# Five of 32 state groups of a selective scan take another route: u replicated by DMA and multiplied on GpSimd, decay in PSUM; products with C two groups at a time

## The chip, the cores and the metric

The kernel runs on one NeuronCore of a Trainium2 chip. The metric is the device time of one launch in microseconds (us). Engines are named as in the profile: PE (TensorE), DVE (VectorE), ACT (ScalarE), POOL (GpSimd) and SP (SyncE, which here only issues DMAs). SPq and ACTq are the DMA issues of SP and ACT.

## What is computed

Two layers follow each other on x of shape 4 x 128 x 64 x 64. The first (attention over 4096 positions and a layer norm) is not touched by the change. The second adds a 3x3 convolution, a spectral convolution and a Mamba block. The change is inside the scan of the Mamba block:

```python
def step(h, inp):                       # one position; h is 256 channels x 16 states
    xt, dtt, Bt, Ct = inp
    dA = jnp.exp(dtt[..., None] * A)
    h = dA * h + dtt[..., None] * Bt[:, None, :] * xt[..., None]
    y = jnp.einsum('bdn,bn->bd', h, Ct)
    return (h, y)
```

With u = dt * x, each of the 256 x 16 = 4096 states h is a recurrence over the positions: h = exp(dt A) h + u B, and y sums h C over the 16 states of a channel.

## The kernel before

The second layer (`layer1`) handles 32 items one after the other: 4 images times 8 chunks (STEPS) of LC = 512 positions. The 4096 states of an item are 32 groups g = 0 to 31 of 128 rows: 8 channels (GC) times 16 states (ST). For each group the engines do this, in this order of dependence:

- SP, `load_dt` (L959): a DMA reads the 8 rows of dt of the group from DRAM (`dt_dram`) and writes each of them to 16 partitions, 256 KB into one of 16 buffers of `d_a` (NDA).
- ACT, `decay` (L1207): d_a = exp(a_neg * d_a), in place, in SBUF.
- PE, `repeat_u` (L1098): one matmul spreads the 8 rows of u to 128 rows in one of 4 PSUM banks (NU).
- DVE, `times_b` (L1255): that bank times B, in place.
- DVE, the scan (L1269): hh = scan of d_a and the bank, into one of 8 buffers (NHH). It reads one operand in SBUF and one in PSUM.
- ACT, `last_state` (L1200): the last column is kept for the next chunk.
- POOL (L1300): hc = hh * c_rep, into one of 8 buffers (NHC).
- PE, `sum_states` (L1080): for four groups at a time, sums over the states into PSUM.

Each engine has its own list written out by hand, and they meet only at semaphores. DVE's order is times_b(g + 1), scan(g), times_b(g + 2), scan(g + 1) and so on. Between the groups each engine also does `prepare`: the projections, activations and tables of item it + 1. On POOL these are ux = dt * xs at g = 13 (L1287), lo_u at g = 17 (L1291) and two gates per item (L1282). u goes to PE as a high and a low part: `hi_u`, and `lo_u`, which ACT places by two DMAs (`place_low`, L1148) into the other half of the partitions of `s_u`.

SP's list per item, step t = 0 to 31, waits for scan t and then issues the load of group t + 16 (for t of 16 and more, group t - 16 of the next item). At t = 16 it first stores dt of the next item to DRAM (`store_dt`, L953, 512 KB) and waits until that has landed before the next load (L957). At t = 6 and 8 it loads the next chunks of the layer's input (`za`, `stage_j`, `zp`), and at t = 18 it stores an output chunk (L948). The last item also issues the 16 loads that a further item would need, and SP's list ends with a wait for all DMAs.

Of the kernel before, what the change touches and what calls it, by code (L numbers as in the profile page):

```python
# [7 lines left out]
ACT = mybir.ActivationFunctionType  # L8
# [745 lines left out]
def layer1(nc, z_ext, w, out, nb=B):  # L754
# [13 lines left out]

    NIT = nb * STEPS
    dt_dram = nc.dram_tensor("dt_dram", [2, INNER, LC], F32, kind="Internal").ap()  # L770
    with ExitStack() as ctx:
        def sb(name, shape, dt=F32):
            return ctx.enter_context(nc.sbuf_tensor(name, shape, dt))
# [51 lines left out]
        d_a = sb("d_a", [128, NDA, LC])  # L825
        hh = sb("hh", [128, NHH, LC])
        hc = sb("hc", [128, NHC, LC])


        loaded, mixed, a_exp, carry_zero, row_zero, halved = [sem(n) for n in (  # L830
# [2 lines left out]
        with nc.Block() as block:  # L833
# [27 lines left out]
            def _(dve):  # L861
# [27 lines left out]
             "hi_ready", "lo_ready", "u_rep", "da_ready", "bu_ready", "scanned", "kept", "hc_ready", "y_done",  # L889
             "y_added", "gated", "z_used", "o_ready", "o_copied", "o_full", "o_even", "o_odd", "dt_stored", "u_placed")]  # L890
        dt_in = [sem(f"dt_in{i}") for i in range(NDA)]


        XS, XD, DT, BI, CI, GATE, GI, NITEM = 0, 2, 3, 5, 6, 7, 9, 10
# [13 lines left out]
        def channels(g):  # L908

            half, jj, i = g // 16, g // 4 % 4, g % 4  # L910
            return 128 * half + 32 * i + GC * jj

        def steps(prepare, emit, tail):

# [6 lines left out]
        with nc.Block() as block:  # L921
            @block.sync
            def _(sp):
                def load(j):

                    p, b, lc = j % 2, j % NIT // STEPS, j % STEPS
                    if j >= 2:
                        sp.wait_ge(item, (j - 2) * NITEM + GI + 1)
                    ge(sp, flipped, 2 * j)
                    sp.dma_start(za[:, p, :], z_ext[b, :, bass.ds(lc * LC, HALO)]).then_inc(z_in, 16)  # L930

                    last = (STEPS - 1 - lc) * LC + W
                    sp.dma_start(stage_j[:, 0:ROWS - 1, :], z_ext[b, :, bass.ds(last + W, LC - W)].rearrange("c (h w) -> c h w", w=W)).then_inc(z_in, 16)
                    sp.dma_start(stage_j[:, ROWS - 1, :], z_ext[b, :, bass.ds((STEPS - lc) % STEPS * LC + W, W)]).then_inc(z_in, 16)

                def load_padded(j):

                    p, b, lc = j % 2, j // STEPS, j % STEPS
                    ge(sp, z_used, j - 1)
                    sp.dma_start(zp[:, p, :, 1:W + 1], z_ext[b, :, bass.ds(lc * LC, HALO)].rearrange("c (h w) -> c h w", w=W)).then_inc(zp_in, 16)  # L940

                def store(j, p):
                    b, lc = j // STEPS, j % STEPS
                    if lc == 0:
                        sp.wait_ge(o_full, b + 1)
                    else:
                        sp.wait_ge(o_copied, j + 1)
                    sp.dma_start(out[b, :, bass.ds(lc * LC, LC)], o_sb[:, p, :]).then_inc((o_even, o_odd)[p], 16)  # L948

                def store_dt(j, p):  # L950

                    sp.wait_ge(item_read, j * NITEM + DT + 2)
                    sp.dma_start(dt_dram[p].rearrange("(h q) l -> q h l", h=2), dt[:, :, :]).then_inc(dt_stored, 16)  # L953

                def load_dt(j, p, g):
                    if g == 0:
# [32 lines left out]
                sp.wait_ge(u_placed, 32 * (NIT + 1))  # L989
                sp.wait_ge(o_even, 16 * (NIT // 2))  # L990
                sp.wait_ge(o_odd, 16 * (NIT // 2))
                for i in range(NDA):
                    sp.wait_ge(dt_in[i], 16 * (NIT * G // NDA + 1))
                sp.wait_ge(z_in, 48 * (NIT + 1))

            @block.tensor
            def _(pe):
# [128 lines left out]
            def _(act):  # L1126
# [76 lines left out]
                def decay(it, g):  # L1203

                    s, j = column(g)
                    act.wait_ge(dt_in[g % NDA], it * (16 * G // NDA) + 16 * (g // NDA) + 16)
                    nc.scalar.activation(d_a[:, g % NDA, :], d_a[:, g % NDA, :], ACT.Exp,  # L1207
                                         scale=a_neg[:, s * 8 + j:s * 8 + j + 1]).then_inc(da_ready, 1)
# [33 lines left out]
            def _(dve):  # L1242
# [4 lines left out]

                def times_b(it, p, g):

                    dve.wait_ge(u_rep, it * G + g + 1)  # L1250
                    if g == 0:
                        dve.wait_ge(item_read, it * NITEM + BI + 1)

# [3 lines left out]
                def emit(it, p):  # L1257
                    times_b(it, p, 0)
                    for g in range(G):

                        if g + 1 < G:
                            times_b(it, p, g + 1)
                        s, j = column(g)
                        dve.wait_ge(bu_ready, it * G + g + 1)
                        dve.wait_ge(da_ready, it * G + g + 1)

                        ge(dve, hc_ready, it * G + g - NHH + 1)
                        ge(dve, kept, it * G + g - NHH + 1)
                        nc.vector.tensor_tensor_scan(hh[:, g % NHH, :], d_a[:, g % NDA, :], ps[:, U_BANK + g % NU, :],  # L1269
                                                     carry[:, it % STEPS, s * 8 + j:s * 8 + j + 1], ALU.mult, ALU.add).then_inc(scanned, 1)  # L1270
                        if g == 16 and it and (it - 1) % STEPS == 0:
                            add_row(it - 1, 1 - p)
# [6 lines left out]
            def _(pool):  # L1279
# [4 lines left out]
                def prepare(j, p, g):  # L1284
                    if g == 13:
                        pool.wait_ge(item_read, j * NITEM + DT + 2)
                        pool.tensor_tensor(ux[:, :, :], dt[:, :, :], xs[:, p, :, :], ALU.mult).then_inc(u_prod, 1)  # L1287
                    elif g == 17:
                        pool.wait_ge(hi_ready, j * 3 + 1)
                        ge(pool, u_placed, j * 32)  # L1290
                        pool.tensor_tensor(lo_u[:, :, :], ux[:, :, :], hi_u[:, :, :].bitcast(F32), ALU.subtract).then_inc(lo_ready, 1)  # L1291

                def emit(it, p):
                    for g in range(G):
                        pool.wait_ge(scanned, it * G + g + 1)
                        if g == 0:
                            pool.wait_ge(item_read, it * NITEM + CI + 1)
# [4 lines left out]
                        if g == 22:  # L1302
                            gate(it, p, 0)
                        if g == 6 and it:
                            gate(it - 1, 1 - p, 1)

                def tail():
# [83 lines left out]
```

## Time and profile before

| | before |
|---|---|
| median of 3 runs | 5654.49 us |
| lowest and highest run | 5650.64 and 5657.19 us |
| the profiled execution's own time | 5656.6 us |
| its span in the trace | 5654.8 us |
| granted TensorE clock over the span | 0.983 |
| share of the span: PE, DVE, ACT, POOL | 94%, 88%, 69%, 83% |
| DMA | 549.14 MB, 97 GB/s over the span |

The execution's own time is 1.8 us more than its span. The first layer takes the first two thirds of the span. The second layer's first scan starts at 3825.7 us, and the last DMA of the program is issued at 5650.5 us. The shares are averages over both layers, so they don't tell what limits the second; the stretches of time below do. The DMA share in a stretch is the mean busy share of the core's 16 DMA engines, and it can come out slightly above 1, as packets overlap.

### The profile page before, as it was taken

What the parts mean: (1) busy time and instruction counts of PE and PEld (TensorE: products, weight loads), DVE (VectorE), ACT (ScalarE), POOL (GpSimd) and SP (SyncE); (2) the same over time, 40 slices, a digit from 0 to 9 for tenths busy, and PEclk for the clock granted to TensorE, in tenths of its full rate; (3) what the DMA queues carried; (4) which work ended last, traced back from release to release, by engine and by line L of the source; (5) the groups of instructions that cost most, each with busy time, mean ns of one, the idle gap of its engine ahead of it and who ended that gap; (6) DMA issues with size and microseconds to landing.
All of it is one profiled execution on the core that took longest, in us unless ns stands there. A gap on an engine that the chain in (4) does not pass through costs nothing. (4 is left out here: it accounts for less than half of the span.)

```text
span 5654.8 us, 81519 instructions
## 1 busy us (share of the span) xinstructions
PE 5338.5 (94%) x25264; PEld 2432.7 (43%) x25264; DVE 4949.7 (88%) x7220; ACT 3876.3 (69%) x7513; POOL 4692.7 (83%) x3661
## 2 busy tenths in 40 slices
PE   7999999999999999999999999968888888888888
PEld 3444444444444444444444444423333333333333
DVE  6888888888888888888888888829999999999998
ACT  3666666666666766666666666657777777777776
POOL 4888887888888788888788888747888888888887
PEclk8999999999999999999999999989999999999999
DMA  4111122211111211112211010225555555555555
GB/s 139 36 53 50 37 61 71 60 55 38 46 49 64 79 39 53 45 40 62 64 54 33 18 32 21 67 84 196 186 190 188 188 187 189 186 188 190 186 188 174
DMA packets 337475, 549.14 MB, mean 97 GB/s; under 512 B 76016, under 2 KB 99568, under 8 KB 335600
## 3 DMA queue, kind: packets, MB, share of 16 engines
q1 hardware_dynamic: 327536, 526.62, 28.8%
q10 hardware_dynamic: 9504, 17.31, 1.1%
q8 instruction: 202, 3.31, 0.2%
q14 instruction: 233, 1.91, 0.1%
HBM read 415.10 MB, written 109.84 MB: 93 GB/s over the span
## 5 line engine op out<-in xcount | busy, mean ns | idle before, releaser
L649 DVE TENSOR_REDUCE mpart<-ps 128x1 f32<-128x512 f32 x4096 | 2539.1, 682 | 536.4 <-PE ps L406 535.8
L533 ACT ACTIVATE exps<-ps 128x512 f32<-128x512 f32 x4096 | 2146.8, 600 | 1139.8 <-PE ps L413 1114.1
L406 PE MATMUL ps<-k_st,q_ring 96*128 96x512 f32 x4096 | 1778.2, 435 | 20.2 <-DMA k_st<-qk_split 15.6
L413 PE MATMUL ps<-q_ring,k_st 98*128 98x512 f32 x4096 | 1621.5, 397 | 3.8 <-ACT exps L533 3.4
L1300 POOL TENSOR_TENSOR hc<-hh,c_rep 128x512 f32<-128x512 f32 x1024 | 1295.8, 1278 | 310.8 <-DVE hh L1269 291.8
L1269 DVE TENSOR_TENSOR_SCAN hh<-d_a,carry,ps 128x512 f32<-128x512 f32 x1024 | 1311.9, 1284 | 0.0
L622 POOL TENSOR_TENSOR held<-exps 128x512 f32<-128x512 f32 x768 | 987.7, 1311 | 359.9 <-ACT exps L533 359.9
L406 PEld LDWEIGHTS ps<-k_st,q_ring 96*128 96x128 f32 x4096 | 774.7, 189 | 1136.5 <-DVE mpart L649 685.2
L622 POOL TENSOR_TENSOR sums<-exps 128x512 f32<-128x512 f32 x896 | 1134.5, 1282 | 72.0 <-ACT exps L533 70.0
L424 PE MATMUL ps<-exps,v_ring 128*32 128x512 f32 x8192 | 1092.4, 605 | 0.0
L413 PEld LDWEIGHTS ps<-q_ring,k_st 98*128 98x128 f32 x4096 | 778.3, 190 | 139.7 <-ACT exps L533 18.0
L1098 PE MATMUL ps<-s_u,sel_g 128*128 128x512 f32 x1024 | 573.6, 565 | 219.3 <-DVE hh L1269 213.9
L1255 DVE TENSOR_TENSOR ps<-ps,b_rep 128x512 f32<-128x512 f32 x1024 | 701.5, 688 | 37.0 <-PE ps L1098 37.0
L1207 ACT ACTIVATE d_a<-d_a,a_neg 128x512 f32<-128x512 f32 x1024 | 731.1, 720 | 3.4 <-DMA d_a<-dt_dram 1.4
L1098 PEld LDWEIGHTS ps<-s_u,sel_g 128*128 128x128 f32 x1024 | 193.5, 189 | 824.0 <-DVE hh L1269 689.3
L622 POOL TENSOR_TENSOR second<-exps 128x512 f32<-128x512 f32 x384 | 493.1, 1284 | 56.0 <-POOL sums L622 0.9
L626 POOL TENSOR_TENSOR sums<-sums,second 128x512 f32<-128x512 f32 x384 | 492.2, 1282 | 30.1
L672 DVE TENSOR_REDUCE held_sum<-held 128x128 f32<-128x768 f32 x512 | 482.0, 942 | 6.0 <-POOL held L622 6.0
L1200 ACT COPY carry<-hh 128x1 f32<-128x1 f32 x1024 | 186.1, 182 | 251.3 <-DVE hh L1269 251.3
L424 PEld LDWEIGHTS ps<-exps,v_ring 128*32 128x32 f32 x8192 | 161.3, 108 | 419.4 <-ACT exps L533 364.3
L1014 PE MATMUL ps<-za,wtap 128*128 128x512 f32 x528 | 274.6, 614 | 26.9 <-DMA stage_j<-z_ext 26.9
L1080 PE MATMUL ps<-hc,sel_y 128*32 128x512 f32 x2048 | 293.6, 647 | 5.4 <-POOL hc L1300 5.4
(113 smaller groups left out, 3881.3 us busy)
## 6 DMA issues: line engine op xcount, KB each, us to landing
d_a<-dt_dram SPq DMA_DIRECT2D x1040, 256.0 KB
qk_split<-hilo SPq DMA_DIRECT2D x128, 256.0 KB, 2.3
out_dram<-out_sb SPq DMA_DIRECT2D x128, 256.0 KB, 2.0
heads_in<-out_dram SPq DMA_DIRECT2D x32, 1024.0 KB, 5.2
q_ring<-qk_split SPq DMA_DIRECT2D x384, 64.0 KB, 2.0
k_st<-qk_split SPq DMA_DIRECT2D x45, 512.0 KB, 7.4
dt_dram<-dt SPq DMA_DIRECT2D x33, 512.0 KB, 5.5
s_u<-lo_u ACTq DMA_DIRECT2D x66, 256.0 KB, 5.9
```

Source lines behind the costliest of these rows:

```text
L406: nc.tensor.matmul(d_bank(("max", m, t)), q_ring[0:PARTS, m % 4, 128 * i:128 * i + 128], k_st[0:PARTS, g % 2, chunk(kc)], start=True, stop ...
L413: nc.tensor.matmul(a_bank(("exp", n, t)), k_st[0:SHIFT, n // NCH % 2, 128 * t:128 * t + 128], q_ring[0:SHIFT, n % 4, :], start=True, stop= ...
L424: ins = nc.tensor.matmul(ps[D * i:D * i + D, OUT_BANK, :], v_ring[:, n // NCH % 2, 4 * v + i, :], exps[:, (2 * v + i // 2) % EXPS, CH * (i ...
L533: nc.scalar.activation(exps[:, u % EXPS, CH * half:CH * half + CH], a_bank(("exp", n, t)), ACT.Exp, scale=SCALE).then_inc(a_done, 1)
L622: pool.tensor_tensor(dst, exps[:, u % EXPS, 0:CH], exps[:, u % EXPS, CH:2 * CH], ALU.add).then_inc(summed, 1)
L626: pool.tensor_tensor(unit, unit, second[:, :], ALU.add).then_inc(summed, 1)
L649: nc.vector.tensor_reduce(mpart[:, m % 2, t % 4, t // 4:t // 4 + 1], d_bank(("max", m, t)), AX.X, ALU.max).then_inc(d_done, 1)
L1098: nc.tensor.matmul(ps[:, U_BANK + g % NU, :], sel_g[:, j, :], s_u[:, p, s, :], start=True, stop=True).then_inc(u_rep, 1)
L1207: nc.scalar.activation(d_a[:, g % NDA, :], d_a[:, g % NDA, :], ACT.Exp, scale=a_neg[:, s * 8 + j:s * 8 + j + 1]).then_inc(da_ready, 1)
L1255: nc.vector.tensor_tensor(bu, bu, b_rep[:, p, :], ALU.mult).then_inc(bu_ready, 1)
L1269: nc.vector.tensor_tensor_scan(hh[:, g % NHH, :], d_a[:, g % NDA, :], ps[:, U_BANK + g % NU, :], carry[:, it % STEPS, s * 8 + j:s * 8 + j ...
L1300: pool.tensor_tensor(hc[:, g % NHC, :], hh[:, g % NHH, :], c_rep[:, p, :], ALU.mult).then_inc(hc_ready, 1)
```

## The change

Five groups of each item (SPREAD = 6, 11, 21, 25 and 29) take another route. The other 27 are handled as before.

- SP stores u of the next item to DRAM at t = 19 (`store_u`, 512 KB), and loads each of the five groups' u with `load_u`: 8 rows, each written to 16 partitions, 256 KB into one of 3 buffers `su` (NSU). In form this DMA is that of `load_dt`. The loads are issued at t = 6, 11, 21, 25 and 29. The one at t = 21 is the first for the next item and waits until its u has landed in DRAM.
- POOL multiplies `su` by B in place (`spread_b`), ahead of the product with C that it stands before in POOL's list.
- ACT writes the decay of these groups to the PSUM bank that `repeat_u` would have filled, two steps later in its list than before, after the scan of group g - 4.
- PE leaves out `repeat_u` and DVE leaves out `times_b` for the five. Their scans read the decay from PSUM and u B from SBUF.
- For all groups, POOL's product with C covers two groups (128 x 1024) with c_rep repeated by a zero stride. It starts when the second of the two is scanned, and `hc_ready` counts pairs.
- ux is written only after the previous u is stored.

```diff
+    SPREAD = (6, 11, 21, 25, 29)
+    NSP, NSU = len(SPREAD), 3
 SP
+                def store_u(j, p):
+                    sp.wait_ge(u_prod, j + 1)
+                    sp.dma_start(u_dram[p].rearrange("(h q) l -> q h l", h=2), ux[:, :, :]).then_inc(u_stored, 16)
+                def load_u(m):
+                    j, g = m // NSP, SPREAD[m % NSP]
+                    if j >= NIT:
+                        return
+                    sp.wait_ge(u_stored, j * 16 + 16)
+                    if m >= NSU:
+                        sp.wait_ge(scanned, (m - NSU) // NSP * G + SPREAD[(m - NSU) % NSP] + 1)
+                    c = channels(g)
+                    sp.dma_start(su[:, m % NSU, :], u_dram[j % 2, c:c + GC, :].rearrange("c (o l) -> c o l", o=1).to_broadcast([GC, ST, LC])
+                                 ).then_inc(su_in[m % NSU], 16)
...
+                        if t == 19:
+                            store_u(it + 1, 1 - p)
+                        for m in LOADS.get(t, ()):
+                            load_u(it * NSP + m)
...
+                LOADS = {SPREAD[0]: (3,), SPREAD[1]: (4,), SPREAD[2]: (5,), SPREAD[3]: (6,), SPREAD[4]: (7,)}
...
                 for g in range(NDA):
                     load_dt(0, 0, g)
+                store_u(0, 0)
+                for m in range(NSU):
+                    load_u(m)
 PE
-                    pe.wait_ge(hc_ready, it * G + 4 * n + 4)
+                    pe.wait_ge(hc_ready, it * G // 2 + 2 * n + 2)
...
-                        repeat_u(it, p, g)
+                        if g not in SPREAD:
+                            repeat_u(it, p, g)
 ACT
+                    if g in SPREAD:
+                        act.wait_ge(scanned, it * G + g - NU + 1)
+                        nc.scalar.activation(ps[:, U_BANK + g % NU, :], d_a[:, g % NDA, :], ACT.Exp,
+                                             scale=a_neg[:, s * 8 + j:s * 8 + j + 1]).then_inc(spread_da, 1)
...
-                        decay(it, g)
+                        if g not in SPREAD:
+                            decay(it, g)
...
+                        if g - 2 in SPREAD:
+                            decay(it, g - 2)
 DVE
-                        if g + 1 < G:
+                        if g + 1 < G and g + 1 not in SPREAD:
                             times_b(it, p, g + 1)
...
+                        a, bu = d_a[:, g % NDA, :], ps[:, U_BANK + g % NU, :]
+                        if g in SPREAD:
+                            m = spread(it, g)
+                            dve.wait_ge(spread_bu, m + 1)
+                            dve.wait_ge(spread_da, m + 1)
+                            a, bu = bu, su[:, m % NSU, :]
 POOL
+                def spread_b(it, p, g):
+                    m = spread(it, g)
+                    pool.wait_ge(su_in[m % NSU], 16 * (m // NSU) + 16)
+                    pool.tensor_tensor(su[:, m % NSU, :], su[:, m % NSU, :], b_rep[:, p, :], ALU.mult).then_inc(spread_bu, 1)
...
-                    for g in range(G):
+                    for g in range(1, G, 2):
...
+                        for w in SPREAD:
+                            if (w - 4) // 2 == g // 2:
+                                spread_b(it, p, w)
...
-                        pool.tensor_tensor(hc[:, g % NHC, :], hh[:, g % NHH, :], c_rep[:, p, :], ALU.mult).then_inc(hc_ready, 1)
+                        pool.tensor_tensor(hc[:, g % NHC - 1:g % NHC + 1, :], hh[:, g % NHH - 1:g % NHH + 1, :],
+                                           c_rep[:, p, :].rearrange("p (o l) -> p o l", o=1).to_broadcast([128, 2, LC]), ALU.mult).then_inc(hc_ready, 1)
```

## Rows read from the trace of the kernel before

**Rows 1.** The page: span and the busy time of the engines.

```profile
span 5654.8 us, 81519 instructions
...
PE 5338.5 (94%) x25264; PEld 2432.7 (43%) x25264; DVE 4949.7 (88%) x7220; ACT 3876.3 (69%) x7513; POOL 4692.7 (83%) x3661
```

**Rows 2.** One item's length by windows: the engines, granted clock, DMA share, GB/s.

```profile
core 0: us, PE busy (x) PEld busy (x) DVE busy (x) ACT busy (x) POOL busy (x), PEclk, DMA share, GB/s
4826.50:4883.14 56.64, 50.08 (x181) 20.10 (x180) 56.64 (x65) 42.85 (x89) 47.24 (x37) 0.97 0.58 187
```

**Rows 3.** Timeline of DVE over the end of an item: start, length, operation.

```profile
4842.59 1.27 DVE L1269 TENSOR_TENSOR_SCAN hh<-d_a,carry,ps 128x512 f32<-128x512 f32 x1
4843.77 0.67 DVE L1255 TENSOR_TENSOR ps<-ps,b_rep 128x512 f32<-128x512 f32 x1
4844.36 2.44 DVE L1269 TENSOR_TENSOR_SCAN hh<-d_a,carry,ps 128x512 f32<-128x512 f32 x2
4846.72 1.27 DVE L1255 TENSOR_TENSOR ps<-ps,b_rep 128x512 f32<-128x512 f32 x2
```

**Rows 4.** Timeline of POOL around ux, in an item.

```profile
4815.91 2.37 POOL L1287 TENSOR_TENSOR ux<-dt,xs 128x1024 f32<-128x1024 f32 x1
4818.24 3.73 POOL L1300 TENSOR_TENSOR hc<-hh,c_rep 128x512 f32<-128x512 f32 x3
```

**Rows 5.** What SP waited for, 4100 to 5400 us: total us, times, longest.

```profile
SPq L959 <- DVE hh L1269: 668.2, 613, 4.2
SPq L957 <- DMA dt_dram<-dt: 119.3, 23, 7.2
```

**Rows 6.** The page's DMA issues: count, KB of one, us to landing.

```profile
d_a<-dt_dram SPq DMA_DIRECT2D x1040, 256.0 KB
...
dt_dram<-dt SPq DMA_DIRECT2D x33, 512.0 KB, 5.5
s_u<-lo_u ACTq DMA_DIRECT2D x66, 256.0 KB, 5.9
za<-z_ext SPq DMA_DIRECT2D x33, 320.0 KB, 4.1
zp<-z_ext SPq DMA_DIRECT2D x32, 320.0 KB, 7.1
...
out<-o_sb SPq DMA_DIRECT2D x32, 256.0 KB, 7.3
stage_j<-z_ext SPq DMA_DIRECT2D x33, 224.0 KB, 4.1
...
stage_j<-z_ext SPq DMA_DIRECT2D x33, 32.0 KB, 4.9
```

**Rows 7.** Windows inside one item, columns as in Rows 2; the last two are DMA's.

```profile
4820.00:4821.00 1.00, 1.00 (x3) 0.44 (x3) 1.00 (x2) 1.00 (x3) 1.00 (x2) 1.00 1.02 373
4838.00:4850.00 12.00, 9.84 (x51) 4.92 (x50) 12.00 (x15) 7.43 (x20) 8.53 (x8) 1.00 0.53 200
4823.00:4826.50 3.50, 3.50 (x15) 1.21 (x14) 3.50 (x5) 0.55 (x2) 3.50 (x3) 1.00 0.13 46
4826.50:4853.50 27.00, 24.02 (x100) 10.95 (x99) 27.00 (x32) 20.41 (x45) 21.89 (x18) 1.00 0.58 197
4854.50:4861.50 7.00, 5.91 (x21) 2.18 (x20) 7.00 (x9) 6.93 (x13) 5.46 (x5) 1.00 0.47 147
```

**Rows 8.** Timeline of SP's DMA issues around the store of dt.

```profile
4818.77 0.47 SPq L953 DMA_DIRECT2D dt_dram<-dt  x1
4824.80 1.21 SPq L959 DMA_DIRECT2D d_a<-dt_dram  x2
```

**Rows 9.** The start of the scans: SP's first loads and DVE's first scan.

```profile
3810.91 25.55 SPq L959 DMA_DIRECT2D d_a<-dt_dram  x22
...
3825.74 1.27 DVE L1269 TENSOR_TENSOR_SCAN hh<-d_a,carry,ps 128x512 f32<-128x512 f32 x1
```

**Rows 10.** The last DMA issue of the program, by SP's timeline.

```profile
5650.48 0.35 SPq L948 DMA_DIRECT2D out<-o_sb  x1
```

More of the change, by code:

```diff
@@ L770, in layer1 @@
     dt_dram = nc.dram_tensor("dt_dram", [2, INNER, LC], F32, kind="Internal").ap()
+    u_dram = nc.dram_tensor("u_dram", [2, INNER, LC], F32, kind="Internal").ap()
+    SPREAD = (6, 11, 21, 25, 29)
+    NSP, NSU = len(SPREAD), 3
     with ExitStack() as ctx:
@@ L827, in layer1 @@
         hc = sb("hc", [128, NHC, LC])
+        su = sb("su", [128, NSU, LC])
         loaded, mixed, a_exp, carry_zero, row_zero, halved = [sem(n) for n in (
@@ L891, in layer1 @@
         dt_in = [sem(f"dt_in{i}") for i in range(NDA)]
+        su_in = [sem(f"su_in{i}") for i in range(NSU)]
+        u_stored, spread_da, spread_bu = [sem(x) for x in ("u_stored", "spread_da", "spread_bu")]
         XS, XD, DT, BI, CI, GATE, GI, NITEM = 0, 2, 3, 5, 6, 7, 9, 10
@@ L911, in channels, with by_pe, spread @@
             return 128 * half + 32 * i + GC * jj
+        def by_pe(it, g):
+            return it * (G - NSP) + g - sum(1 for w in SPREAD if w < g)
+        def spread(it, g):
+            return it * NSP + SPREAD.index(g)
         def steps(prepare, emit, tail):
@@ L989, in _ @@
                 sp.wait_ge(u_placed, 32 * (NIT + 1))
+                sp.wait_ge(u_stored, 16 * (NIT + 1))
                 sp.wait_ge(o_even, 16 * (NIT // 2))
@@ L1206, in decay @@
                     act.wait_ge(dt_in[g % NDA], it * (16 * G // NDA) + 16 * (g // NDA) + 16)
-                    nc.scalar.activation(d_a[:, g % NDA, :], d_a[:, g % NDA, :], ACT.Exp,
-                                         scale=a_neg[:, s * 8 + j:s * 8 + j + 1]).then_inc(da_ready, 1)
+                    if g in SPREAD:
+                        act.wait_ge(scanned, it * G + g - NU + 1)
+                        nc.scalar.activation(ps[:, U_BANK + g % NU, :], d_a[:, g % NDA, :], ACT.Exp,
+                                             scale=a_neg[:, s * 8 + j:s * 8 + j + 1]).then_inc(spread_da, 1)
+                    else:
+                        nc.scalar.activation(d_a[:, g % NDA, :], d_a[:, g % NDA, :], ACT.Exp,
+                                             scale=a_neg[:, s * 8 + j:s * 8 + j + 1]).then_inc(da_ready, 1)
                 def emit(it, p):
                     for g in range(G):
-                        decay(it, g)
+                        if g not in SPREAD:
+                            decay(it, g)
                         if g >= KEEP:
@@ L1248, in times_b @@
                 def times_b(it, p, g):
-                    dve.wait_ge(u_rep, it * G + g + 1)
+                    dve.wait_ge(u_rep, by_pe(it, g) + 1)
                     if g == 0:
@@ L1259, in emit @@
                     for g in range(G):
-                        if g + 1 < G:
+                        if g + 1 < G and g + 1 not in SPREAD:
                             times_b(it, p, g + 1)
                         s, j = column(g)
-                        dve.wait_ge(bu_ready, it * G + g + 1)
-                        dve.wait_ge(da_ready, it * G + g + 1)
-                        ge(dve, hc_ready, it * G + g - NHH + 1)
+                        a, bu = d_a[:, g % NDA, :], ps[:, U_BANK + g % NU, :]
[4 more added lines that the diff above has]
+                            a, bu = bu, su[:, m % NSU, :]
+                        else:
+                            dve.wait_ge(bu_ready, by_pe(it, g) + 1)
+                            dve.wait_ge(da_ready, by_pe(it, g) + 1)
+                        if it * G + g >= NHH:
+                            dve.wait_ge(hc_ready, (it * G + g - NHH) // 2 + 1)
                         ge(dve, kept, it * G + g - NHH + 1)
-                        nc.vector.tensor_tensor_scan(hh[:, g % NHH, :], d_a[:, g % NDA, :], ps[:, U_BANK + g % NU, :],
+                        nc.vector.tensor_tensor_scan(hh[:, g % NHH, :], a, bu,
                                                      carry[:, it % STEPS, s * 8 + j:s * 8 + j + 1], ALU.mult, ALU.add).then_inc(scanned, 1)
@@ L1286, in prepare @@
                         pool.wait_ge(item_read, j * NITEM + DT + 2)
+                        ge(pool, u_stored, j * 16)
                         pool.tensor_tensor(ux[:, :, :], dt[:, :, :], xs[:, p, :, :], ALU.mult).then_inc(u_prod, 1)
@@ L1291, in prepare @@
                         pool.tensor_tensor(lo_u[:, :, :], ux[:, :, :], hi_u[:, :, :].bitcast(F32), ALU.subtract).then_inc(lo_ready, 1)
+                def spread_b(it, p, g):
+                    m = spread(it, g)
+                    pool.wait_ge(su_in[m % NSU], 16 * (m // NSU) + 16)
+                    pool.tensor_tensor(su[:, m % NSU, :], su[:, m % NSU, :], b_rep[:, p, :], ALU.mult).then_inc(spread_bu, 1)
                 def emit(it, p):
-                    for g in range(G):
+                    for g in range(1, G, 2):
+                        if g == 1:
+                            pool.wait_ge(item_read, it * NITEM + CI + 1)
+                        for w in SPREAD:
+                            if (w - 4) // 2 == g // 2:
+                                spread_b(it, p, w)
                         pool.wait_ge(scanned, it * G + g + 1)
-                        if g == 0:
-                            pool.wait_ge(item_read, it * NITEM + CI + 1)
                         ge(pool, y_done, it * 8 + (g - NHC) // 4 + 1)
-                        pool.tensor_tensor(hc[:, g % NHC, :], hh[:, g % NHH, :], c_rep[:, p, :], ALU.mult).then_inc(hc_ready, 1)
+                        pool.tensor_tensor(hc[:, g % NHC - 1:g % NHC + 1, :], hh[:, g % NHH - 1:g % NHH + 1, :],
+                                           c_rep[:, p, :].rearrange("p (o l) -> p o l", o=1).to_broadcast([128, 2, LC]), ALU.mult).then_inc(hc_ready, 1)
                         prepare(it + 1, 1 - p, g)
-                        if g == 22:
+                        if g == 23:
                             gate(it, p, 0)
-                        if g == 6 and it:
+                        if g == 7 and it:
                             gate(it - 1, 1 - p, 1)
```

## The prediction, made before the changed kernel ran

> **What bounds the kernel now.** I read the page first, then cut the second layer into stretches of one item, then followed single queues. On the page PE leads with 94%, but that mixes two layers [rows 1]. In one item of the second layer, 56.64 us, the row says something else: DVE is busy for 56.64 of 56.64 us, PE for 50.08, POOL for 47.24 and ACT for 42.85 [rows 2]. The reader is to see DVE without a hole and nobody else so. The timeline of DVE shows the pace: from the start of a scan to the start of the next times_b is 4843.77 - 4842.59 = 1.18 us, from there to the next scan 4844.36 - 4843.77 = 0.59 us. Together 1.77 us a group, and 32 x 1.77 = 56.6 us an item. Two scans in a row, which occur at the end of an item, start 2.44 - 1.27 = 1.17 us apart, so a scan costs 1.18 us whatever follows it [rows 3].
>
> The view that decides is that of the DMA engines, though. While only loads of d_a run, they move 200 GB/s at a share of 0.53; while the store of dt runs beside them, 373 GB/s at a share of 1.02 [rows 7]. I read this so: a load of d_a uses 8 of the 16 DMA engines, all of them fully, and that half can do no more than 200 GB/s. A load of 262,144 bytes then costs 1.31 us of that half. It has 8 source rows. The Trainium skill says why, on its page "DMA: Bandwidth & Descriptors", section "Why a DMA increments its semaphore by 16 and not by 1": a transfer is split over the largest number of engines up to 16 that divides the slowest dimension of both sides, which is 8 here. By this rule the trace's half share is the full rate of such a load.
>
> **The busy half of the DMA engines, before.** Per item it gets all of the 32 loads, 32 x 256 = 8192 KB, and half of what else moves: dt 512, za 320, zp 320, stage_j 224 + 32, out 256 and s_u 2 x 256, so 2176 / 2 = 1088 KB [rows 6]. That is 9280 KB = 9.50 MB, or 47.5 us at 200 GB/s. A stretch of an item shows what this misses: from 4826.5 to 4853.5 us, 27.0 us, the mean share is 0.58, over the 0.53 of a full half, and 197 x 27.0 = 5.32 MB move [rows 7]. Out and s_u are in it, 768 KB = 0.79 MB, half of it on the other engines, so the busy half carries 4.93 MB, 24.6 us at 200 GB/s. It took 2.4 us longer. With that the item's work is 47.5 + 2.4 = 49.9 us.
>
> To it comes a forced hole. SP issues the store of dt at 4818.77 and the next load at 4824.80 [rows 8], after waiting for the landing; 23 items of a long stretch lose 119.3 / 23 = 5.2 us of SP in this wait [rows 5]. In the 3.5 us from 4823.0 to 4826.5 the share is 0.13 [rows 7], a hole of 3.5 x (1 - 0.13 / 0.53) = 2.6 us. The half is full again by 4826.5, so packets come at most 1.7 us after the issue at 4824.80; I take 1.3. So the half is taken for 49.9 + 2.6 = 52.5 of 56.64 us. From above: after 4854.5 loads run at 147 GB/s, DVE's pace of one in 1.77 us, idle for 7 x (1 - 147 / 200) = 1.85 us [rows 7]; 56.64 - 1.85 - 2.6 = 52.2 us of work is thus the most there can be. SP's wait for scans, 668.2 us in 1300 [rows 5], only says that SP isn't the limit; it issues, and the work piles up behind it.
>
> **The change part by part.**
> DVE loses five times_b per item, 5 x 0.59 = 2.95 us, 53.7 us are left [rows 3]. The operands of the five scans change places, still one in SBUF and one in PSUM; I take the scan's price as unchanged.
> PE loses five matmuls and was 6.6 us under DVE; no cost.
> POOL, by start to start: a product takes 1.24 us ((3.73 - 1.27) / 2), ux 2.33 us (4818.24 - 4815.91) [rows 4]. The trace has no product with a repeated operand. Below it is bounded by ux's 2.33 us for 1024 columns, above by two single products, 2.48; I take 2.33, as it has the same count of elements. POOL's item becomes 16 x 2.33 + 5 x 1.24 (spread_b) + 2 x 1.24 (gates) + 2 x 2.33 (ux, lo_u) = 50.6 us, at most 53.0. Either is under 53.7. Its backlog is longest after ux, lo_u and three spread_b: from group 13 to 25 it has six pairs 14.0, ux and lo_u 4.7, gate 1.2 and three spread_b 3.7, 23.6 us, while DVE takes 12 x 1.77 - 2 x 0.59 = 20.1 us. So it is some 3.5 us behind; hh and hc have 8 buffers, over 10 us. Hidden.
> ACT writes five decays to PSUM rather than SBUF, same count; it has 13.8 us free per item. Hidden.
> DMA gains five loads of 256 KB on the busy half and a store of 512 KB, half of it there: 1536 KB = 1.57 MB, 7.9 us per item. The new wait for u's landing has two loads issued behind the store (t = 20 and 21), 2.6 us of work, about the time from the store's last packet to the next load's first; I price this second hole at 0, and at most 2.6.
>
> **The sum.** The busy half needs 49.9 + 7.9 + 2.6 = 60.4 us per item. That is above DVE's 53.7 and above the 56.64 of before. The loads, not the scans, then set the pace: SP falls behind the scans, decays wait for d_a, scans for decays. Bounds: without the 2.4 us 57.9 ; with the most work 52.2 + 7.9 + 2.6 = 62.7.
> Now the whole. The first loads are issued at 3810.91 [rows 9], packets from 3812.2. Then 16 loads 21.0, s_u 1.3, store of u 1.3, a hole 2.6, three loads of u 3.9: the items' loads begin at 3842.3. 31 items of 60.4 make 1872.4. The last has no loads of z and three of u less: 60.4 - 2.3 - 3.9 = 54.2. That is 5768.9; the useless loads at the end count too, since SP waits for them. From the last issue to the end of the span were 4.3 us [rows 1, 10]; I add 3, as the last load is issued before its turn. Span 5771.9, its own time 1.8 more, 5773.7, against 5656.6 of the profiled run: +117. The profiled run was 2.1 above the median, so 5771.6; I say 5770. By the bounds: 57.9 gives 31 x 2.5 + 2.5 = 80 less, 5690; 62.7 gives 74 more, 5844.
>
> **The rivals.**
> DVE stays the bound, the other sign. This is so if loads of u cost the busy half little, that is if the half isn't a hard limit: the point from which it decides is 53.7 us of DMA per item, 6.7 less than my sum. For it: nobody waits for d_a now, and SP mostly waits for scans. Against it: 12 us at exactly 200 GB/s while DVE's pace asks for 148. It gives 32 x 2.95 = 94.4 less. At the start u of group 6 lands late: 3812.2 + 21.0 + 1.3 + 1.3 + 2.6 + 1.3 and about 0.5, plus 1.24 on POOL, is 3841.4, while the scan was due at 3825.74 + 6 x 1.77 - 0.59 = 3835.8: 5.6 more. At the end the last pair starts with its second group, 1.1 + 1.1 more. 5654.5 - 94.4 + 5.6 + 2.2 = 5568. The same DMA page, "Specifications", gives a fabric ceiling of 435 GB/s over 16 engines. As an estimate from it, an item's 12.4 MB (all of the KB above, with the change's) would need 29 us, and this rival would hold. The trace's 200 GB/s of loads alone speaks against its use here.
> DMA is the bound, but lighter: the hole is filled and the 2.4 us aren't there. 47.5 + 7.9 = 55.4 us an item: 1.2 under before, 5654.5 - 38 = about 5615.
> POOL is the bound: it would need a pair of over 2.52 us to pass 53.7, ((53.7 - 13.3) / 16), and over 2.94 to pass 60.4. At 2.7 us alone it would be 56.5 us, no change. Both inputs and the count speak against it.
>
> **How the numbers follow.** DMA as the bound, between 57.9 and 62.7 us an item: 0.74. DVE as the bound: 0.13. Light DMA: 0.08, spread on both sides of no change, 0.04 faster, 0.03 the same, 0.01 slower. POOL: 0.05, split 0.02, 0.02 and 0.01. A measurement of this kernel tells 0.2%, 11 us, from no change. Faster 0.13 + 0.04 + 0.02 = 0.19, same 0.03 + 0.02 = 0.05, slower 0.74 + 0.01 + 0.01 = 0.76. The likeliest case's own range is 5690 to 5844. The range for all reaches down to 5640, which leaves out the DVE case and a part of the others.
>
> **What would show it.** If right: DVE's busy share in an item falls below 0.95, with waits of its scan for ACT's decay (or POOL's su), and ACT waits for the DMA of d_a; SP's wait for scans nearly goes; the DMA share is over 0.55 everywhere but in one hole per item; an item takes some 60 us; scan to scan at a skipped times_b is 1.18 us. A d_a load alone still shows 200 GB/s. It is wrong if DVE is at 1.00 and an item takes 53.7 us; or if the loads of u show the 8 engines above 200 GB/s; or if POOL's pair lasts over 2.9 us.

## The result: 4.6% slower, and the profile after

The changed kernel takes 5910.34 us (median of 4 runs, 5898.96 to 5922.98), the kernel before 5652.84 in the same comparison: a ratio of 1.0455, 95% interval 1.0425 to 1.0485. The profiled execution took 5922.98 us, at the upper end. The forecast was 5770, with 5844 as its upper end. The direction was right and so was the mechanism. The size was not: some 116 us of loss were forecast, less than half of the 257 measured.

The page of the changed kernel, to be read beside [rows 1, 6]; of the DMA issues the first line is the load of d_a, the second the new load of u:

```profile
span 5921.2 us, 80727 instructions
...
PE 5384.0 (91%) x25104; PEld 2441.2 (41%) x25104; DVE 4878.3 (82%) x7060; ACT 3877.2 (65%) x7513; POOL 4796.1 (81%) x3309
...
DMA 13%; issue 3%; DVE 2%; ACT 1%; SPq 1%; PE 1%; POOL 0%; DVEq 0%; POOLq 0%; ACTq 0%
DMA d_a<-dt_dram 12%; DVE hh L1326 2%; DMA dt_dram<-dt 1%; SPq L989 1%; DVE ps L1304 1%; ACT d_a L1253 0%; POOL hc L1366 0%; ACT L1176 0%; ACT L1175 0%; ACT xs L1175 0%; PE ps L1126 0%; PE ps L1119 0%; ACT ps L1250 0%; ACT carry L1240 0%; SPq L962 0%
...
d_a<-dt_dram SPq DMA_DIRECT2D x1040, 256.0 KB
su<-u_dram SPq DMA_DIRECT2D x160, 256.0 KB
...
dt_dram<-dt SPq DMA_DIRECT2D x33, 512.0 KB, 14.0
```

In the second layer no engine is full any more, as the windows below show; the page's 91% for PE is raised by the first layer. The chain that ended last (the second pair of lines) runs through the DMA of d_a for 12% of the span. The store of dt lands after 14.0 us where it took 5.5 [rows 6]: it stands behind the loads issued before it.

Windows of the changed kernel, columns as in [rows 2, 7]:

```profile
4100.00:5400.00 1300.00, 1028.10 (x3487) 408.25 (x3486) 1085.61 (x1179) 856.29 (x1752) 1010.97 (x498) 0.89 0.58 192
5008.00:5024.00 16.00, 10.56 (x31) 3.70 (x32) 10.83 (x14) 11.95 (x24) 12.91 (x8) 0.79 0.52 201
5044.50:5045.50 1.00, 1.00 (x8) 0.55 (x4) 1.00 (x2) 0.81 (x2) 1.00 (x1) 1.00 1.06 408
5053.50:5058.50 5.00, 0.99 (x5) 0.40 (x3) 1.98 (x3) 2.71 (x6) 2.09 (x2) 0.81 0.17 57
```

DVE is busy for 1085.6 of 1300 us, 0.84, where it was at 1.00 [rows 2]. In the second row 16 us of loads run at 201 GB/s and a share of 0.52, the ceiling of [rows 7], while DVE stands still for a third of the time. In the third the store of dt fills the other half of the engines. The last is the hole after the wait for dt's landing: 5 x (1 - 0.17 / 0.53) = 3.4 us without work. SP issued the store at 5042.80 and the next load only at 5056.87. An item now takes 65.2 us in the mean. SP's timeline shows the load of za, one per item, first and last of 23 in a long stretch:

```profile
4037.86 1.10 SPq L944 DMA_DIRECT2D za<-z_ext  x1
...
5473.12 1.10 SPq L944 DMA_DIRECT2D za<-z_ext  x1
```

(5473.12 - 4037.86) / 22 = 65.24. Single items differ: from one load of za to the next it is 62.8 to 70.4 us, with a median of 64.3. Who waits for whom from 4100 to 5400 us (us in total, times, longest), and below it SP's own waits:

```profile
ACT d_a L1253 <- DMA d_a<-dt_dram: 436.6, 335, 4.3
...
DVE hh L1326 <- issue: 181.1, 66, 6.2
...
POOL su L1354 <- DMA su<-u_dram: 103.5, 40, 5.0
```

```profile
SPq L987 <- DMA dt_dram<-dt: 263.6, 20, 13.8
SPq L989 <- DVE hh L1326: 255.8, 271, 5.7
SPq L982 <- DMA u_dram<-ux: 112.7, 20, 6.4
```

ACT waits 436.6 us for d_a, which it waited 1.4 us for in the whole second layer before. SP's wait for dt's landing went from 5.2 us a time [rows 5] to 263.6 / 20 = 13.2. What DVE waits for shows in its timeline and POOL's, at group 6 of an item:

```profile
5007.94 0.67 DVE L1304 TENSOR_TENSOR ps<-ps,b_rep 128x512 f32<-128x512 f32 x1
5012.67 1.28 DVE L1326 TENSOR_TENSOR_SCAN hh<-ps,carry,su 128x512 f32<-128x512 f32 x1 [4.05 <-issue]
5013.87 0.67 DVE L1304 TENSOR_TENSOR ps<-ps,b_rep 128x512 f32<-128x512 f32 x1
```

```profile
5007.32 1.27 POOL L1354 TENSOR_TENSOR su<-su,b_rep 128x512 f32<-128x512 f32 x1 [3.51 <-DMA su<-u_dram]
5008.55 4.65 POOL L1366 TENSOR_TENSOR hc<-hh,c_rep 128x1024 f32<-128x1024 f32 x2
```

POOL had u B of the group ready at 5008.6, so the scan at 5012.67 waited for its decay. ACT's timeline shows why that was late:

```profile
5009.88 0.72 ACT L1253 ACTIVATE d_a<-d_a,a_neg 128x512 f32<-128x512 f32 x1 [3.05 <-DMA d_a<-dt_dram]
5011.19 0.72 ACT L1253 ACTIVATE d_a<-d_a,a_neg 128x512 f32<-128x512 f32 x1 [0.51 <-DMA d_a<-dt_dram]
5011.90 0.68 ACT L1250 ACTIVATE ps<-d_a,a_neg 128x512 f32<-128x512 f32 x1
```

The decay of group 6 (L1250) stands behind those of groups 7 and 8 in ACT's list, and both waited for their loads of d_a. So most of DVE's idle time falls before the five scans (181.1 of some 214 us in the waits above). That tells where the wait shows, not what causes it: the experiments below tell the two apart. The scan itself lasts 1.28 us with its operands exchanged, as before.

### The profile page after: what moved, and what is told of

Same layout as the page of the kernel before. It is cut to its first block and busy times, and to the rows that moved or that the text cites. A ratio compares the mean times of both kernels' runs of the same rounds, so it can differ in the third digit from the quotient of the medians.

```text
span 5921.2 us, 80727 instructions
## 1 busy us (share of the span) xinstructions
PE 5384.0 (91%) x25104; PEld 2441.2 (41%) x25104; DVE 4878.3 (82%) x7060; ACT 3877.2 (65%) x7513; POOL 4796.1 (81%) x3309
## 2 busy tenths in 40 slices
DMA packets 368206, 608.34 MB, mean 103 GB/s; under 512 B 77824, under 2 KB 101376, under 8 KB 366336
## 5 line engine op out<-in xcount | busy, mean ns | idle before, releaser
L1366 POOL TENSOR_TENSOR hc<-hh,c_rep 128x1024 f32<-128x1024 f32 x512 | 1205.8, 2365 | 279.7 <-DVE hh L1326 278.7
L622 POOL TENSOR_TENSOR sums<-exps 128x512 f32<-128x512 f32 x896 | 1133.4, 1282 | 72.5 <-ACT exps L533 70.4
L1326 DVE TENSOR_TENSOR_SCAN hh<-d_a,carry,ps 128x512 f32<-128x512 f32 x864 | 1082.0, 1268 | 14.8 <-DVE ps L1304 9.8
L1253 ACT ACTIVATE d_a<-d_a,a_neg 128x512 f32<-128x512 f32 x864 | 621.3, 721 | 665.4 <-DMA d_a<-dt_dram 662.1
L1137 PE MATMUL ps<-s_u,sel_g 128*128 128x512 f32 x864 | 549.8, 638 | 190.0 <-DVE hh L1326 176.9
L1304 DVE TENSOR_TENSOR ps<-ps,b_rep 128x512 f32<-128x512 f32 x864 | 580.6, 675 | 73.5 <-PE ps L1137 73.5
L1137 PEld LDWEIGHTS ps<-s_u,sel_g 128*128 128x128 f32 x864 | 169.9, 197 | 670.6 <-DVE hh L1326 520.7
L1326 DVE TENSOR_TENSOR_SCAN hh<-ps,carry,su 128x512 f32<-128x512 f32 x160 | 204.8, 1280 | 275.3 <-issue 264.4
L1354 POOL TENSOR_TENSOR su<-su,b_rep 128x512 f32<-128x512 f32 x160 | 203.9, 1274 | 168.9 <-DMA su<-u_dram 168.9
L1119 PE MATMUL ps<-hc,sel_y 128*32 128x512 f32 x2048 | 325.8, 714 | 7.3 <-POOL hc L1366 7.3
```

The lines of the kernel that those rows point to most:

```text
L622: pool.tensor_tensor(dst, exps[:, u % EXPS, 0:CH], exps[:, u % EXPS, CH:2 * CH], ALU.add).then_inc(summed, 1)
L1137: nc.tensor.matmul(ps[:, U_BANK + g % NU, :], sel_g[:, j, :], s_u[:, p, s, :], start=True, stop=True).then_inc(u_rep, 1)
L1304: nc.vector.tensor_tensor(bu, bu, b_rep[:, p, :], ALU.mult).then_inc(bu_ready, 1)
L1326: nc.vector.tensor_tensor_scan(hh[:, g % NHH, :], a, bu, carry[:, it % STEPS, s * 8 + j:s * 8 + j + 1], ALU.mult, ALU.add).then_inc(scanne ...
L1366: pool.tensor_tensor(hc[:, g % NHC - 1:g % NHC + 1, :], hh[:, g % NHH - 1:g % NHH + 1, :], c_rep[:, p, :].rearrange("p (o l) -> p o l", o= ...
```

## The experiments

Each gives its ratio to the kernel before on the same chip, with a 95% interval.

**Is it DMA or the new order of work?** Two kernels divide the change. The first has all of it but the DMAs (the ones at the start, not shown, are left out too):

```diff
-                        if t == 19:
-                            store_u(it + 1, 1 - p)
-                        for m in LOADS.get(t, ()):
-                            load_u(it * NSP + m)
...
-                    pool.tensor_tensor(su[:, m % NSU, :], su[:, m % NSU, :], b_rep[:, p, :], ALU.mult).then_inc(spread_bu, 1)
+                    pool.tensor_tensor(su[:, m % NSU, :], win[:, :], b_rep[:, p, :], ALU.mult).then_inc(spread_bu, 1)
```

> The changed kernel without the store of u and the five loads of u per item; spread_b multiplies a constant tile by B instead, so the five groups' u is wrong. Theory (the busy half of the DMA engines is the bound, 64.1 us an item in the changed kernel): its work falls by 7.9 us to some 52.5 plus a hole of 2.6 to 3.7, about 56, so DMA and DVE (53.7) are nearly level: 5561 if DVE alone sets the pace, up to 5640 if DMA still does. Rival (the new order of work on POOL, ACT and DVE makes DVE wait, whatever DMA does): stays above 5800.

Measured 5611.42 us (5589.33 to 5622.35), ratio 0.9923 (0.9901 to 0.9946). It is faster than before, but above what DVE alone would give. ACT still waits 200.0 us in 1300 for d_a (row below), so the busy half is nearly full even without u. DVE is idle for 33.4 us of these 1300, 12.1 of them for a matmul of PE, a wait that comes back below. (The 64.1 us of the expectation was a first reading of the item's length; the mean is 65.2.)

```profile
ACT d_a L1245 <- DMA d_a<-dt_dram: 200.0, 173, 3.2
```

The second has the DMAs alone, added to the kernel before, with `store_u` and `load_u` as in the change:

```diff
...
+                        if t == 19:
+                            store_u(it + 1, 1 - p)
+                        for m in LOADS.get(t, ()):
+                            load_u(it * NSP + m)
```

> The kernel before with nothing but the DMAs added: u stored to DRAM, and five loads per item into buffers that nobody reads. Theory (DMA bound): the full price, as in the changed kernel, 5890 to 5920, with DVE waiting for d_a. Rival (the loss comes from the compute side): no change, 5653.

Measured 5904.11 us (5902.58 to 5911.61), ratio 1.0451 (1.0433 to 1.0468). Data that nobody reads costs 251 us, nearly all of the change's 258. In its windows DVE is down to 0.89, and ACT waits 412.3 us for d_a:

```profile
4100.00:5400.00 1300.00, 1055.80 (x3640) 424.52 (x3639) 1157.11 (x1298) 877.30 (x1783) 958.67 (x728) 0.91 0.58 194
```

```profile
ACT d_a L1241 <- DMA d_a<-dt_dram: 412.3, 390, 4.2
```

**Is it the eight engines?** Rows of dt and u are stored twice, side by side, so that a load has 16 source rows:

```diff
-                    sp.dma_start(dt_dram[p].rearrange("(h q) l -> q h l", h=2), dt[:, :, :]).then_inc(dt_stored, 16)
+                    for r in range(2):
+                        sp.dma_start(dt_dram[p, :, r, :].rearrange("(h q) l -> q h l", h=2), dt[:, :, :]).then_inc(dt_stored, 16)
...
-                    sp.dma_start(d_a[:, g % NDA, :], dt_dram[p, c:c + GC, :].rearrange("c (o l) -> c o l", o=1).to_broadcast([GC, ST, LC])
+                    sp.dma_start(d_a[:, g % NDA, :], dt_dram[p, c:c + GC, :, :].rearrange("c r (o l) -> (c r) o l", o=1).to_broadcast([2 * GC, ST // 2, LC])
```

The edit for u is the same.

> The changed kernel with dt and u each stored twice to DRAM (each row beside its copy), so that a load reads 16 rows and writes each to 8 partitions instead of 8 rows to 16. Theory (a load of 8 rows uses 8 of the 16 DMA engines): a load alone runs at some 400 GB/s and a share of 1, the busiest engines have 60.4 - 37 x 0.65 + 2.7 = 39 us of work per item, DVE sets the pace at 53.7 us, 5561 to 5575. Rival (200 GB/s is the limit of such loads whatever the engines): 1 MB more per item, so 5910 or slower.

Measured 5594.96 us (5592.15 to 5596.07), ratio 0.9899 (0.9884 to 0.9913): 315 us less than the changed kernel, though it moves more bytes. The windows of this variant, first a stretch of loads:

```profile
5031.00:5037.00 6.00, 5.46 (x19) 1.76 (x18) 6.00 (x7) 3.73 (x9) 5.20 (x4) 1.00 1.06 276
5043.00:5050.00 7.00, 4.78 (x11) 1.84 (x14) 7.00 (x8) 3.28 (x9) 6.42 (x4) 0.76 1.13 267
```

The share is 1.06 where an 8-row load has 0.53, so all 16 engines work. But they move 276 GB/s, not 400: 0.95 us a load rather than 0.65. The time, too, is some 20 us above the 5561 to 5575 that was expected; "A version that beats both" finds the reason.

The same in the kernel before, where DVE has no hole to give back:

> The kernel before with dt stored twice and loads of 16 rows. Theory: DVE is the bound before, so no change, 5653 within 0.2%, while loads in the trace show 400 GB/s and the backlog goes. Rival (DMA already costs the kernel before something): faster by more than 0.2%.

Measured 5650.62 us (5647.66 to 5651.68), ratio 0.9995 (0.9986 to 1.0004): no change. So the loads' rate cost the kernel before nothing; it had just enough of it. The loads don't reach the expected 400 GB/s here either. Catching up after the store of dt they move 276:

```profile
4884.00:4887.00 3.00, 3.00 (x21) 2.44 (x19) 3.00 (x5) 2.08 (x6) 2.16 (x3) 1.00 1.00 276
```

**Do the two copies side by side hold the 16-row load back?** The changed kernel with loads of 16 different neighbouring rows, without copies:

```diff
-                    c = channels(g)
+                    c = min(channels(g), INNER - 2 * GC)
-                    sp.dma_start(d_a[:, g % NDA, :], dt_dram[p, c:c + GC, :].rearrange("c (o l) -> c o l", o=1).to_broadcast([GC, ST, LC])
+                    sp.dma_start(d_a[:, g % NDA, :], dt_dram[p, c:c + 2 * GC, :].rearrange("c (o l) -> c o l", o=1).to_broadcast([2 * GC, ST // 2, LC])
```

The edit for u is the same.

> The changed kernel with loads that read 16 neighbouring rows, 8 partitions each, without doubled rows in DRAM: each group gets other channels' dt and u, so the scan's input is wrong. With the doubled rows a 16-row load ran at 276 GB/s and a share of 1.06, 0.95 us each, instead of the 400 GB/s expected from twice the engines. If it is the two copies lying side by side that slows it, this load reaches 350 GB/s or more; if all 16 engines writing to 128 partitions (or reading one place) is the limit, again some 275. Time: as the doubled variant, some 5595, with 1 MB less to store per item.

One run, 5591.04 us. Among the first loads its trace has this window:

```profile
3820.00:3826.00 6.00, 5.71 (x14) 3.18 (x14) 4.91 (x7) 3.33 (x9) 0.44 (x1) 0.73 1.05 282
```

282 GB/s, so the copies aren't what limits it. Single stretches vary, between 255 and 306 GB/s for the most part. Over all stretches of 3 us with a share over 1 and packets of this size alone the median is 273 here and 271 with doubled rows. What limits the load stays open. This kernel differs from the changed one only in the rows of its 1040 + 160 loads, and its page confirms the count of engines. The changed kernel's row comes first:

```profile
DMA packets 368206, 608.34 MB, mean 103 GB/s; under 512 B 77824, under 2 KB 101376, under 8 KB 366336
DMA packets 377806, 608.37 MB, mean 109 GB/s; under 512 B 87424, under 2 KB 110976, under 8 KB 375936
```

It has 87424 - 77824 = 9600 more packets under 512 bytes, 8 for each of the 1200 loads, at the same bytes. In the trace they are of 4 bytes, which fits one for each engine that takes part, 16 a load instead of 8.

**The terms of the sum.** Three edits of the changed kernel, each taking one thing from the busy half. The changed kernel's own runs span 24 us, so each difference is good to some 12 us, 0.4 us an item. First the hole, by storing dt earlier:

```diff
-                        if t == G - NDA:
+                        if t == G - NDA - 3:
                             store_dt(it + 1, 1 - p)
```

> The changed kernel with the store of dt at t = 13 instead of 16, so that three loads are issued behind it before SP waits for its landing. Theory (the hole after the wait is forced idle time of the bound resource, 3.7 us per item in the changed kernel's trace): the hole closes, 32 x 3.7 = 118 us less, 5790. Rival (the hole only moves, or something else fills its time): 5880 or more.

Measured 5768.65 us (5766.18 to 5773.31), ratio 1.0204 (1.0189 to 1.022): 142 us less than the changed kernel, 4.4 us an item. Its DMA moves 206 GB/s over the long stretch instead of 192, and DVE is at 0.89:

```profile
4100.00:5400.00 1300.00, 1057.63 (x3748) 425.70 (x3749) 1155.95 (x1265) 915.38 (x1883) 1083.40 (x535) 0.94 0.61 206
```

Not all of the 4.4 us is the hole. Added up over windows of half a microsecond with a share under 0.4, the half stands idle for 3.2 us an item in the changed kernel (mean of 22 items) and for 0.6 here, 2.6 less. What is left of the hole here is behind the wait for u's landing. The other 1.8 us are work that got cheaper. In the changed kernel the store of dt (issued at 5042.80) and the two DMAs of s_u (at 5044.66) move together, and load packets of 2,048 bytes beside s_u take 124 ns in the mean; here the store is earlier, and they take 103. That this accounts for the 1.8 us is argued, not shown.

Then the load of zp, in 256-byte pieces, left out from the third item on:

```diff
-                        if t == 8 and it + 1 < NIT:
+                        if t == 8 and it == 0:
```

> The changed kernel with zp loaded for the first two items only, so the 3x3 convolution of the others has wrong input. My sum priced this load by its bytes, 320 KB / 2 at 200 GB/s = 0.82 us an item: 26 us less, 5884. If its pieces of 256 bytes cost the busy half more than their bytes, up to 3 us an item: 95 us less, 5815.

Measured 5843.24 us (5836.64 to 5863.81), ratio 1.0342 (1.0322 to 1.0361): 67 us less than the changed kernel, 2.1 us an item, two and a half times the price by bytes. The packets agree: one of 256 bytes takes 22 ns in the mean (median 18), where a load's packet of 2,048 bytes takes 84 in the median, and the 1280 pieces of zp over 16 engines make 80 x 22 ns = 1.8 us. Then the two DMAs of u's low part:

```diff
+                        if j < 2:
                             act.dma_start(s_u[b, p, part::2, :].bitcast(F32), lo_u[a, :, :].bitcast(F32)).then_inc(u_placed, 16)
```

> The changed kernel with the low part of u placed by DMA for the first two items only, so the others' low part is stale. My sum priced these two DMAs by their bytes, 1.31 us an item: 42 us less, 5868. If a copy from SBUF to SBUF holds the engines longer than its bytes say, or is what slows the loads beside it, up to 3.7 us: 118 us less, 5792.

Measured 5809.61 us (5802.43 to 5811.98), ratio 1.0272 (1.0255 to 1.0289): 101 us less, 3.1 us an item, again over twice the bytes' 1.31. A part can be read off the changed kernel's page, where these 66 DMAs have a queue of their own:

```profile
q10 hardware_dynamic: 9504, 17.31, 1.1%
```

1.1% of 5921.2 us over 33 pairs is 2.0 us of every engine. The rest fits the slower load packets beside them (124 ns against 92 elsewhere), though no run shows that alone.

**The compute side.** The kernel before with products two groups at a time and nothing else (the last part of the change's diff, and with it POOL's two gates, which stand one group later, as in the changed kernel):

> The kernel before with only the products with C taken two groups at a time. POOL's pair was priced at 2.33 us; the changed kernel shows 2.365 busy, 2.33 start to start. DVE stays the bound at 56.64 us an item: no change but 1 to 2 us at the end (the last pair starts later), 5654 to 5656. If PE's or DVE's waits for pairs cost something in the loop: 5665 or more.

Measured 5664.58 us (5659.77 to 5669.35), ratio 1.0014 (1.0005 to 1.0024), 8.5 us more. I expected 1 to 2, and the time is nearly the 5665 that stood for waits in the loop. POOL's pair is priced right, 2.368 us:

```profile
L1301 POOL TENSOR_TENSOR hc<-hh,c_rep 128x1024 f32<-128x1024 f32 x365 | 864.4, 2368 | 279.3 <-DVE hh L1270 252.6 <-PE ps L1080 24.1
```

```profile
4100.00:5400.00 1300.00, 1134.62 (x4102) 461.23 (x4100) 1297.85 (x1463) 975.37 (x2007) 1020.66 (x456) 0.98 0.57 187
```

The loss is in the loop: from the first scan to the end of the last it is 1823.5 us against 1814.8 before, 8.7 more, and only some 1 us comes after the last scan. DVE's waits are 2.15 us in these 1300, some 3 in all. Another 3.6 us are in an instruction of DVE that runs once per image, the addition of a row to o_sb, 64 columns with both inputs in SBUF. It lasted 1.06 us before and lasts 1.95 now (medians of 4). The first row is POOL's product, the second this addition:

```profile
4367.67 2.37 POOL L1301 TENSOR_TENSOR hc<-hh,c_rep 128x1024 f32<-128x1024 f32 x1
4368.15 1.97 DVE L1246 TENSOR_TENSOR o_sb<-o_sb,row 128x64 f32<-128x64 f32 x1
```

It ends at 4370.12, just behind POOL's product at 4370.04. That is no accident of this one: in eight of the runs, four times each, it ends some 0.1 us after the product or other instruction that POOL was in when it began, and lasts anything from 0.20 to 2.34 us. DVE's scans and products with B, which have an operand in PSUM, keep their 1.27 and 0.67 us beside POOL. The other 2 us of the 8.7 I did not find.

**A version that beats both.** With doubled rows one wait of DVE is left, 15.4 us in the 1300 (19 times, up to 0.8). PE's timeline shows where it comes from:

```profile
5043.91 0.50 PE L1139 MATMUL ps<-s_u,sel_g 128*128 128x512 f32 x1 [0.81 <-DVE hh L1328]
5045.82 2.07 PE L1128 MATMUL ps<-yt,wout 128*128 128x512 f32 x2 [1.41 <-POOL yt L1341]
5046.90 1.41 PE L1139 MATMUL ps<-s_u,sel_g 128*128 128x512 f32 x1
5048.11 1.58 PE L1128 MATMUL ps<-yt,wout 128*128 128x512 f32 x2
5049.63 1.06 PE L1121 MATMUL ps<-hc,sel_y 128*32 128x512 f32 x8
5050.62 0.50 PE L1139 MATMUL ps<-s_u,sel_g 128*128 128x512 f32 x1
5050.96 1.02 PE L1073 MATMUL ps<-xd,wdt 128*128 128x512 f32 x2
```

```profile
5042.19 2.35 POOL L1368 TENSOR_TENSOR hc<-hh,c_rep 128x1024 f32<-128x1024 f32 x1
5044.50 1.26 POOL L1341 TENSOR_TENSOR yt<-yt,gz 128x512 f32<-128x512 f32 x1
```

```profile
5051.16 0.70 DVE L1306 TENSOR_TENSOR ps<-ps,b_rep 128x512 f32<-128x512 f32 x1 [0.82 <-PE ps L1139]
```

The output projection (L1128) waits 1.41 us for POOL's gate (L1341), which stands behind a product of two groups. PE was idle for 0.81 and 1.41 us before it, and from 5046 to 5049 the granted clock is 0.50, the lower of its two levels, 1.2 GHz. A pair of matmuls takes 2.07 us there, and 1.02 behind it at the full 2.4 GHz (L1073). What stands behind the pair comes 0.82 us late for DVE. One line moves the gate:

```diff
-                        if g == 7 and it:
+                        if g == 5 and it:
                             gate(it - 1, 1 - p, 1)
```

> The variant with doubled rows of dt and u (16-row loads), and POOL's second gate moved from behind the product of groups 6 and 7 to behind that of 4 and 5. In the trace of the doubled variant DVE waits once per item, 0.8 us, for a matmul that stands behind the output projection, which waits for that gate. Theory (that chain is what keeps it from 53.7 us an item): 5595 - 26 = 5569. Rival (the wait moves to the next late product): no change, 5595.

Measured 5572.39 us (5570.3 to 5574.84), ratio 0.9856 (0.9842 to 0.9871). The wait is gone but for one of 0.6 us, the median matmul of the projection takes 592 ns instead of 1055, and DVE is full:

```profile
4100.00:5400.00 1300.00, 1149.88 (x4220) 457.13 (x4212) 1299.44 (x1427) 1030.15 (x2118) 1220.29 (x603) 1.00 0.91 251
```

Two more variants of it:

> The best variant so far (doubled rows, gate after groups 4 and 5) with the store of dt at t = 13 as well. Its DVE is busy for 1299.4 of 1300 us, so theory (DVE is the bound, DMA no longer): no change from 5572. If the hole still cost it something: up to 10 us less.

5571.32 us (5569.86 to 5576.06), ratio 0.985 (0.9836 to 0.9865): no change, the hole costs nothing where DMA isn't the bound.

> Doubled rows for dt alone: u is stored once, and its five loads have 8 rows each; gate and store of dt as in the variant before. Busiest engines per item, from the runs: 32 x 0.95 + 5 x 1.31 and some 12 of other work, about 49 us, under DVE's 53.7. Theory: no change from 5572. Rival (loads of u late for POOL): slower by 10 us or more.

5572.44 us (5571.67 to 5575.32), ratio 0.9852 (0.9837 to 0.9866): no change either. It is enough that the 32 loads of dt use all the engines. Nor do the loads of u come late for POOL.

## Why the prediction had the mechanism and missed the size

- **DVE's gain.** 0.59 us per skipped times_b and a scan of 1.18 us whatever its operands: right. From load of za to load of za the last version's item takes 53.65 us, as 32 x 1.77 - 5 x 0.59 says. The rival "DVE stays the bound" was worked out as 5568; where the experiments made it true, the kernel took 5572. Its late start is there too: 6.63 us of wait for u of group 6 in the first item, where 5.6 were worked out.
- **The busy half of the DMA engines as the bound.** Right, and shown from both sides: its DMAs alone bring 251 us of loss, and with 16-row loads the loss turns into a gain.
- **PE, ACT, POOL hidden.** Right in the changed kernel, where all wait for DMA. Without the DMA bound POOL's lateness is not quite hidden: 0.8 us in most items, by the gate, 5594.96 - 5572.39 = 23 us. POOL's longer products also cost some 9 us in the kernel before, where I had counted 2. The sum had compared POOL's lateness with the depth of hh and hc, and not with the matmuls behind the gate on PE.
- **The sum, 60.4 us an item against 65.2.** This is the step that failed: what the busy half has to do per item, and its hole, were priced too low. The sum had 57.8 us of work and 2.6 of hole. The trace has some 3.2 us of hole in the mean, and so some 62 of work: about 4.2 of the missing 4.8 us are work. The 2.4 us over the bytes came from a stretch that holds loads, out and s_u; za, zp and the store of dt lie outside it and stayed at their bytes. By the experiments: zp was 0.82 us and measured 2.1. For s_u the bytes' 1.31 and the 2.4 make 3.7, measured 3.1, so this one was covered. The store of dt with the wait behind it was worth 4.4 against the 2.6 of the hole. The new DMAs, 7.9 us by bytes, cost (5910.34 - 5611.42) / 32 = 9.3 or more, since the kernel without them is held by DVE for part of the time. Together 1.3 - 0.6 + 1.8 + 1.4 = 3.9. The terms were measured one at a time and need not add up. Of the 0.9 that is left, 0.4 is that the profiled run is 12.6 us above the median; 0.5 stays open, no more than the error of one term. The second hole, behind the wait for u's landing, was priced at 0, and rightly: from 4998 to 5003 us, while SP waits in it, the share is 0.53.
  I had an upper bound for the work of before from above, 52.2, which takes in every transfer, but took the estimate from bytes, 49.9, and then left the hole and the price of the new bytes without an upper end. With 52.2, 9.3 and a hole of 3.2 the sum is 64.7. The range was too narrow for that. (Its lower bound, 60.4 - 2.4, is 58.0 and not 57.9, which changes nothing.)
- **Start and end.** From the first load of za, 3847.40, to the last, 5797.10, 30 items take 65.0 us in the mean, and 31 x 4.6 = 142 us is most of the 149 that the span is above my 5771.9. Loads of u are issued at 3838.58 and the first item's loads behind them; the forecast start of 3842.3 is about 1.5 us early. From the last issue to the end of the span the trace has 5921.2 - 5908.3 = 12.9 us where the sum took 3: the loads that nobody needs drain first. Some 4 us the other way lie in the last item, which I didn't take apart.
- **What should have shown.** DVE under 0.95, ACT's waits for d_a and one hole per item: as said. A share over 0.55 everywhere else: wrong, it is 0.52 for 16 us where loads run alone, and 0.58 only in the mean. SP's wait for scans, which I said nearly goes, is still 255.8 us. SP issues four loads in 2.42 us (from 5007.08) where the busy half needs 5.2, so it soon meets the scan that has to free the next of the 16 buffers, and from then on it issues at DMA's pace, nine in 12.35 us (from 5010.59). A queue's issuer waits for buffers also where the queue is the bound; that reading was wrong.

## What to carry to other kernels

Look at a stretch in which one kind of transfer runs alone, and see whether its rate is above what the consumer asks for: that is a full resource even at a DMA share of 0.53, and nobody waits for it yet. Count then what a change adds to that half, with the pieces and holes at what they cost rather than at their bytes. Here a layout with 16 source rows raised the rate of a load from 200 to 276 GB/s over one with 8. Where a store is waited for, issue a few loads behind it first.

## What the runs showed of the hardware that was not expected

- Twice the DMA engines didn't double the rate of a broadcast load: 8 engines 201 GB/s (25 each), 16 engines some 270 to 280 GB/s (17 to 18 each), with doubled or with different source rows.
- Two DMAs from SBUF to SBUF of 256 KB each cost a kernel bound by DMA 3.1 us; a load of 320 KB in 256-byte pieces 2.1 us. By bytes at the same rate they would be 1.31 and 0.82.
- A wait for a store's landing in front of the next load left the busy half idle for 3.2 us a time. Three loads issued behind the store brought that to 0.6, and the whole move gained 4.4.
- A DVE addition of 64 columns with both inputs in SBUF lasted until the instruction that POOL was in had ended, 32 times of 32 in eight runs: 1.06 us in the kernel before, 1.95 with products of two groups. DVE instructions with an operand in PSUM showed no such thing.
